# Two query tiles interleaved through attention, output projection and layer norm of an eight-core transformer layer

## The chip, the cores and the metric

The kernel runs on 8 cores of one Trainium2 chip, all with the same program and different data: core c takes batch entry c // 2 and four of its eight 512-row query tiles (the even cores tiles 0, 3, 4, 7, the odd ones 1, 2, 5, 6). The cores exchange nothing. The metric is the device time of the slowest core in microseconds (us).

## The reference

```python
# x: (4, 4096, 2048); tiers of 4, 8 and 12 heads of 64
Q_all = x @ W_Q
K_all = x @ W_K
V_all = x @ W_V
# tiers 0 and 1 add a low-rank term of rank 8 a head to K and V
scores = jnp.einsum('bhqd,bhkd->bhqk', Qh, Kh) / jnp.sqrt(jnp.float32(dk))
scores = jnp.where(causal, scores, jnp.float32(-1e+30))
attn = jax.nn.softmax(scores, axis=-1)
out = jnp.einsum('bhqk,bhkd->bhqd', attn, Vh)
a = jnp.concatenate(head_outs, axis=-1) @ W_O
x = _layernorm(x + a, axis=-1)
h = jax.nn.silu(x @ w_gate) * (x @ w_up)
x = _layernorm(x + _sparsify_2to4(h) @ w_down, axis=-1)
```

The weights are block-triangular, so that an output block of `W_O` takes only 2, 6 or 12 of the 12 head pairs. `_sparsify_2to4` keeps the two largest of each four hidden values.

## The kernel before

The program is one list of instructions for each engine, written out by Python loops. `kb.emit(engine, ..., waits, inc)` appends an instruction to its engine's list with the semaphore values that it waits for; `Buf` objects hold who wrote and who read a buffer, and give these waits. Each engine runs its list in order, so the order of the `emit` calls is the order of work. A DMA is an entry in the list of SyncE (SP) or GpSimd (POOL): it waits there, and what stands behind it in that list waits too.

Stages, with barriers between the first and second and the second and third:

1. K, V and Q for all heads by TensorE, written to HBM (`kspill`, `vspill`, `qspill`), and `wo` copied there as bf16 (`wospill`).
2. For each own tile `s` of four: attention, output projection with the residual `xTo`, layer norm (`_emit_ln`) into `x1`. Tile `s` sees `EXT[s]` = 2, 4, 6, 8 key blocks of 512. This is what the change rewrites.
3. The feed-forward part in two blocks of 1024 rows (L746 and L756 gate and up, L873 down), and the second layer norm.

Attention of a tile runs over 12 head pairs `hp` of 128 rows. A head pair is `ext` x 4 steps of 128 keys. A step is: two score matmuls (L524 and L532, one for each head, on the upper and lower 64 rows), one exp of 128x1024 on ScalarE (L547), for the last eight steps of the head pair two mask products on VectorE (L559), and two AV matmuls (L578) that add into banks 6 and 7. Their 65 rows hold 64 of the head's output and the sum of the exps.

Scores rotate through three pairs of PSUM banks (0 to 5), the exps through three buffers (`e3`). A step's AV is put in a queue, `avq`, and emitted when more than two are in it:

```python
                    avq.append(do_av)
                    if len(avq) > 2:
                        flush_av()
            while avq:
                flush_av()
```

So AV of step k - 2 stands behind the scores of step k in TensorE's list, and the scores of step k + 1 behind that. At the end of a head pair the queue is emptied, and a fixed chain follows (the hand-over): VectorE copies banks 6 and 7 (L602, L606), ScalarE takes Ln and exp(-x) of the sums (L612, L616, L622, L626), TensorE spreads the result over 128 rows (L635, L641) into the next score pair, and VectorE multiplies (L649, L656) into `ob`. The first scores of the next head pair stand behind L641 in TensorE's list.

K and V of a head pair are loaded into `kst` and `vst`, two buffers each, so that the next head pair's are on their way; Q of all heads of a tile comes in one load (`qb`), and `xTo` of the tile goes to `xos` through POOL's queue as soon as the layer norm before has been read. All loads are emitted by the helper at L230.

The output projection (L686) takes two groups of eight 128-row output blocks, one PSUM bank each. Each group runs over the head pairs `ho` with one `wospill` load of 512 KB (128x2048) into one of two slots: 6 loads for the first group, 12 for the second. VectorE then adds the eight banks to `xos` (L699). The layer norm takes sums over 16 blocks (L960, L976 on TensorE, L967 on VectorE), a short chain on one row, and 32 VectorE operations (L1072, L1080); its banks are 0 to 3.

## Time and profile before

| | |
|---|---|
| time, median of 2 runs | 6110.39 us (6107.38 to 6113.41) |
| the profiled execution's own time | 6106.46 us |
| its span, slowest core | 6104.9 us (the cores: 6046.4 to 6104.9) |
| mean granted clock of TensorE, slowest core | 0.897 |
| busy in the span: TensorE | 4793.2 us (79%) |
| VectorE | 1844.3 us (30%) |
| ScalarE | 1169.1 us (19%) |
| GpSimd | 440.7 us (7%) |

The span is what the trace covers; 1.6 us of the execution's own time lie around it. Busy time says how long an engine had an instruction running, not whether anybody waited for it. The stage that is changed runs from about 1101 to 2951 us of the span. "<-" in a row's brackets names who ended the idle time before it. A granted clock of 1.00 is 2.4 GHz, 0.50 is 1.2 GHz. In timeline rows a number after x counts merged instructions.

### The profile page before, as it was taken

How to read it: one execution, taken by the hardware profiler on the slowest of the kernel's cores; microseconds unless marked ns; L12 is line 12 of the kernel's file. 1: busy time of each engine (PE TensorE's matmuls, PEld its weight loads, DVE VectorE, ACT ScalarE, POOL GpSimd, SP SyncE). 2: the span in 40 equal slices, each digit the busy share in tenths (PEclk: the TensorE clock that was granted, in tenths of full speed). 3: DMA queues.
4: the chain of work that ended last, by engine and by line, in shares of the span. 5: the costliest groups of instructions: out<-in, count | busy, mean ns of one | idle time of the engine just before them, and what ended most of it. 6: DMA issues, size and time to landing. Idle time of an engine off the chain costs nothing.

```text
span 6104.9 us, 61933 instructions; the slowest of 8 cores (6046.4 to 6104.9 us)
## 1 busy us (share of the span) xinstructions
PE 4793.2 (79%) x20400; PEld 1825.8 (30%) x20400; DVE 1844.3 (30%) x2803; ACT 1169.1 (19%) x1301; POOL 440.7 (7%) x811
## 2 busy tenths in 40 slices
PE   0889896465766766886799999788849999978894
PEld 0333333011111111111244444333314444433331
DVE  0211212434333223222444455100045445530004
ACT  0000000434626754884000000000000000000000
POOL 0000000000000000000000000122200000012220
PEclk9999998676778887988799999899969999989996
DMA  9232335322132123112344454689824455558893
GB/s 155 48 59 49 63 60 128 85 85 58 41 107 56 42 73 97 49 49 76 62 91 96 97 97 97 138 179 186 186 69 97 90 97 97 97 110 185 180 196 95
DMA packets 363871, 598.92 MB, mean 98 GB/s; under 512 B 85872, under 2 KB 208944, under 8 KB 360496
## 3 DMA queue, kind: packets, MB, share of 16 engines
q0 software_dynamic: 157488, 260.75, 27.5%
q1 hardware_dynamic: 206080, 334.21, 17.7%
q8 instruction: 180, 2.95, 0.2%
q14 instruction: 123, 1.01, 0.1%
HBM read 767.26 MB, written 88.28 MB: 140 GB/s over the span
## 4 chain that ended last, share of the span: by engine, by line
PE 52%; DMA 17%; DVE 13%; ACT 8%; issue 6%; another core or an unknown queue 2%; DVEq 0%; ACTq 0%; SPq 0%; POOLq 0%; POOL 0%
PE ps L746 15%; PE ps L756 15%; DMA ar<-wd 8%; PE ps L873 8%; ACT ar L547 6%; DMA vspill<-ar 6%; PE ps L343 4%; DVE ar L559 4%; PE ps L578 3%; DMA ar<-wospill 2%; PE ps L436 2%; PE ps L524 2%; PE ps L976 1%; PE ps L686 1%
## 5 line engine op out<-in xcount | busy, mean ns | idle before, releaser
L746 PE MATMUL ps<-ar 128*128 128x512 bf16 x4096 | 1221.4, 380 | 60.6 <-DMA ar<-wg 31.2
L756 PE MATMUL ps<-ar 128*128 128x512 bf16 x4096 | 1221.0, 380 | 1.1 <-DMA ar<-wu 1.1
L873 PE MATMUL ps<-ar 128*128 128x512 bf16 x4096 | 938.8, 385 | 195.8 <-DMA ar<-wd 122.9
L547 ACT ACTIVATE ar<-ps 128x1024 bf16<-128x1024 f32 x960 | 911.4, 1067 | 290.7 <-PE ps L532 231.7
L578 PE MATMUL ps<-ar 128*65 128x512 bf16 x1920 | 647.3, 422 | 136.1 <-DVE ar L559 135.0
L873 PEld LDWEIGHTS ps<-ar 128*128 128x128 bf16 x4096 | 391.4, 99 | 743.1 <-issue 326.1
L524 PE MATMUL ps<-ar 64*128 64x512 bf16 x960 | 419.3, 447 | 191.8 <-DMA ar<-kspill 82.1
L746 PEld LDWEIGHTS ps<-ar 128*128 128x128 bf16 x4096 | 401.3, 98 | 547.1 <-issue 65.7
L559 DVE TENSOR_TENSOR ar<-ar 128x512 bf16<-128x512 bf16 x768 | 318.1, 425 | 811.1 <-ACT ar L547 768.8
L756 PEld LDWEIGHTS ps<-ar 128*128 128x128 bf16 x4096 | 401.3, 98 | 486.9 <-issue 5.3
L776 ACT ACTIVATE ar<-ps 128x1024 bf16<-128x1024 f32 x128 | 131.1, 1024 | 1609.0 <-PE ps L746 953.0
L532 PE MATMUL ps<-ar 64*128 64x512 bf16 x960 | 420.3, 448 | 0.0
L279 DVE CAST ar<-ps 128x512 bf16<-128x512 f32 x240 | 164.8, 692 | 673.6 <-DMA vspill<-ar 386.1
L891 DVE TENSOR_TENSOR ar<-ps,ar 128x512 bf16<-128x512 f32 x64 | 44.3, 692 | 1056.9 <-PE ps L873 1050.7
L230 POOL DMA_DIRECT2D ar<-wd x512 | 270.6, 529 | 903.3 <-PE ps L873 758.4
L781 DVE TENSOR_SCALAR ar<-ar 128x1024 bf16<-128x1024 bf16 x128 | 56.6, 442 | 847.4 <-ACT ar L776 847.4
L524 PEld LDWEIGHTS ps<-ar 64*128 64x128 bf16 x960 | 87.5, 95 | 665.0 <-issue 665.0
L373 PE MATMUL ps<-ar 128*128 128x512 bf16 x1184 | 271.2, 379 | 0.0
L578 PEld LDWEIGHTS ps<-ar 128*65 128x65 bf16 x1920 | 142.4, 115 | 427.9 <-issue 427.9
L343 PE MATMUL ps<-ar 128*128 128x512 bf16 x1056 | 237.7, 380 | 0.0
L230 POOL DMA_DIRECT2D ar<-wg x128 | 67.9, 530 | 2299.9 <-PE ps L756 1707.3
L1010 ACT ACT_TABLE_LOAD x2 | 2.6, 1283 | 1191.0 <-DVE sm L1006 1191.0
(103 smaller groups left out, 2671.6 us busy)
## 6 DMA issues: line engine op xcount, KB each, us to landing
ar<-hspill SPq DMA_DIRECT2D x512, 256.0 KB, 4.7
ar<-wg POOLq DMA_DIRECT2D x128, 512.0 KB, 6.0
ar<-wu POOLq DMA_DIRECT2D x128, 512.0 KB, 8.2
ar<-wd POOLq DMA_DIRECT2D x512, 128.0 KB, 4.9
ar<-wospill SPq DMA_DIRECT2D x72, 512.0 KB, 3.4
hspill<-ar SPq DMA_DIRECT2D x128, 256.0 KB, 7.1
ar<-xT POOLq DMA_DIRECT2D x8, 2048.0 KB, 16.9
ar<-xTo POOLq DMA_DIRECT2D x8, 2048.0 KB, 15.9
```

What stands on the lines that cost most here:

```text
L230: return kb.emit(eng, lambda e, o=out_ap, i=in_ap: e.dma_start(out=o, in_=i), waits=waits, inc=sem, incval=16)
L279: lambda e, dst=dst, src=src_bank_ap: e.tensor_copy(dst, src),
L343: lambda e, b=b, m=m, kc=kc, last=last, xch=xch: e.matmul(bank(b), wkb[:, kc * 1536 + m * 128: kc * 1536 + (m + 1) * 128], xch(kc), start= ...
L373: lambda e, b=b, ts=ts, dblk=dblk, kc=kc, xch=xch: e.matmul(bank(b), xch(kc, c0=ts * 128, w=128), wvb[:, kc * 1536 + dblk * 512: kc * 1536 ...
L524: lambda e, b0=b0, sub=sub, j=j, hp=hp, kstg=kstg: e.matmul(bank(b0), kstg[0:64, j * 512 + sub * 128: j * 512 + (sub + 1) * 128], qb[0:64, ...
L532: lambda e, b0=b0, sub=sub, j=j, hp=hp, kstg=kstg: e.matmul(bank(b0 + 1), kstg[64:128, j * 512 + sub * 128: j * 512 + (sub + 1) * 128], qb ...
L547: lambda e, b0=b0, eap=eap: e.activation(eap, ps[:, b0 * 512:(b0 + 2) * 512], AF.Exp, scale=0.125),
L559: lambda e, eap=eap, midx=midx, sub=sub, hd=hd: e.tensor_tensor(eap[:, hd * 512:(hd + 1) * 512], eap[:, hd * 512:(hd + 1) * 512], A(msk_o ...
L578: st=st, ste=ste: e.matmul(bank(6 + hd, rows=65), vstg[:, 130 * c + 65 * hd: 130 * c + 65 * hd + 65], eap[:, hd * 512:(hd + 1) * 512], sta ...
L746: lambda e, bb=bb, th=th, kc=kc, s=s, wgs=wgs: e.matmul(bank(bb + th), wgs[:, kc * 128:(kc + 1) * 128], x1[:, kc * 2048 + s * 512: kc * 20 ...
L756: lambda e, bb=bb, th=th, kc=kc, s=s, wus=wus: e.matmul(bank(bb + 2 + th), wus[:, kc * 128:(kc + 1) * 128], x1[:, kc * 2048 + s * 512: kc ...
L873: lambda e, bi=bi, ft=ft, th=th, ic=ic, wst=wst, hst=hst: e.matmul(bank(bi), wst[:, ft * 128:(ft + 1) * 128], hst[:, th * 512:(th + 1) * 512],
```

## The change

The four tiles are taken as two pairs, tiles 0 and 1, then 2 and 3; the first of a pair is chain A, the second chain B, with key extents 2 and 4, then 6 and 8.

- Attention: for each head pair, K and V are loaded once, for B's extent, and used by both. While A has key blocks left, the steps alternate A, B, A, B. B's last eight steps then run alone (solo). A owns score banks 0 and 1 and output banks 6 and 7, B owns 2 and 3, and 4 and 5; in solo steps B's scores alternate between both score pairs. `avq` is now one for each chain and is emitted when more than one is in it. At the start of the solo steps A's queue is emptied.
- The hand-over, now `_finalize_hp`, is emitted for A and then for B at the end of the head pair, with the same buffers for both (`efin`, `sm32`, `rowb`); B's last AV stands behind A's.
- Q comes for one head pair at a time, two loads of 128x512 in a ring of four. The second chain has its own masks (`msk2`).
- `xTo` of both tiles goes into the space of `kst` and `vst`, so its loads wait until the pair's attention has read these, and the next pair's K and V loads wait until both layer norms have read it.
- Output projection: both tiles together, four groups of four output blocks (eight banks: four for each tile), with 12 `wospill` loads in each group, also where `ho` is past what the group needs.
- Layer norm: A's, then B's, by the same `_emit_ln`.

```diff
+    ob2_o = xos_o
+    xosr_o = kst_o
+    B["ob2"] = Buf()
+    B["msk2"] = Buf()
+    B["qr"] = [Buf() for _ in range(4)]
+    B["xos2"] = Buf()
...
-    for s in range(4):
-        ext = EXT[s]
-        ev = dma("gpsimd", "xos",
-                 xos.rearrange("p (c t) -> p c t", c=NCK),
-                 cm(xTo)[:, :, s * 512:(s + 1) * 512],
-                 waits=B["xos"].wr_waits())
-        B["xos"].note_write(ev)
...
-                   qspill[s].rearrange("h p q -> p h q"),
-                   waits=B["qb"].wr_waits() + B["qspill"].rd_waits())
...
+    for sp_ in range(2):
+        sA, sB = 2 * sp_, 2 * sp_ + 1
+        chains = []
+        for ci, (s, pair, obank, oboff, mB, moff) in enumerate(
+                ((sA, (0, 1), (6, 7), ob_o, "msk", msk_o),
+                 (sB, (2, 3), (4, 5), ob2_o, "msk2", ring_o))):
...
+            c.avq = []
+            chains.append(c)
+        for c in chains:
+            mw = B[c.mB].wr_waits()
+            dma("sync", "mk", A(c.moff, 2048), msk[2 * c.s + 0], waits=mw)
+            dma("sync", "mk", A(c.moff + 2048, 2048), msk[2 * c.s + 1], waits=mw)
...
             kpar = hp % 2
-            kstg = A(kst_o + kpar * 4096, ext * 512)
-            vstg = A(vst_o + kpar * 4160, 130 * 4 * ext)
+            kstg = A(kst_o + kpar * 4096, 4096)
+            vstg = A(vst_o + kpar * 4160, 4160)
...
-            evk = dma("sync", "k%d" % kpar, kstg,
-                      kspill[hp, :, 0:ext * 512],
+            evk = dma("sync", "k%d" % kpar, kstg[:, 0:EXT[sB] * 512],
+                      kspill[hp, :, 0:EXT[sB] * 512],
                       waits=kB.wr_waits() + B["kspill"].rd_waits())
...
-            avq = []
-
-            def flush_av():
-                fn = avq.pop(0)
-                fn()
-
-            for j in range(ext):
...
+            dma("sync", "ql%d" % qsl, qstg[:, 0:512], qspill[sA, hp], waits=qw)
+            dma("sync", "ql%d" % qsl, qstg[:, 512:1024], qspill[sB, hp], waits=())
...
+            def chain_step(c, j, sub, pair, kstg=kstg, vstg=vstg, kB=kB, vB=vB,
+                           qstg=qstg, qrB=qrB, hp=hp):
+                b0 = pair[0]
+                qoff = 0 if c.s % 2 == 0 else 512
+                w = (kB.rd_waits() + qrB.rd_waits()
+                     + B["bank"][b0].wr_waits() + B["bank"][b0 + 1].wr_waits())
...
+                er = erot[0] % 3
...
+                if j >= c.ext - 2:
+                    midx = j - (c.ext - 2)
...
+                def do_av(c=c, j=j, sub=sub, eB=eB, eap=eap, vstg=vstg, vB=vB):
+                    cc = 4 * j + sub
...
+                c.avq.append(do_av)
+                if len(c.avq) > 1:
+                    c.avq.pop(0)()
...
+            cA, cB = chains
+            for j in range(cB.ext):
                 for sub in range(4):
-                    pr = prot[0] % 3
-                    prot[0] += 1
-                    b0 = 2 * pr
-                    w = (kB.rd_waits() + B["qb"].rd_waits()
-                         + B["bank"][b0].wr_waits() + B["bank"][b0 + 1].wr_waits())
...
-                    avq.append(do_av)
-                    if len(avq) > 2:
-                        flush_av()
-            while avq:
-                flush_av()
...
-        for grp in range(2):
-            fms = list(range(8 * grp, 8 * grp + 8))
-            nho = 6 if grp == 0 else HPN
-            for ho in range(nho):
...
+                    if j < cA.ext:
+                        chain_step(cA, j, sub, cA.pair)
+                    solo = j >= cA.ext
+                    if solo and j == cA.ext and sub == 0:
+                        while cA.avq:
+                            cA.avq.pop(0)()
+                    pair = cB.pair if (not solo or (j * 4 + sub) % 2 == 0) \
+                        else cA.pair
+                    chain_step(cB, j, sub, pair)
+            for c in chains:
+                while c.avq:
+                    c.avq.pop(0)()
+                _finalize_hp(kb, B, A, bank, kb_cnt=None, c=c, hp=hp,
+                             e_o=e_o, sm32=sm32, rowb=rowb, onesr=onesr, AFv=AF,
+                             ALUv=ALU)
+
...
+        xosbufs = (A(xosr_o, NCK * 512), A(vst_o, NCK * 512))
...
+            xB = xBs[ci]
+            kvw = (B["kst"][0].wr_waits() + B["kst"][1].wr_waits()) if ci == 0 \
+                else (B["vst"][0].wr_waits() + B["vst"][1].wr_waits())
+            evxo = dma("gpsimd", "xos" if ci == 0 else "xos2",
+                       xosbufs[ci].rearrange("p (cc t) -> p cc t", cc=NCK),
+                       cm(xTo)[:, :, c.s * 512:(c.s + 1) * 512],
+                       waits=xB.wr_waits() + kvw)
+            xB.note_write(evxo)
+        for grp4 in range(4):
+            fms = list(range(4 * grp4, 4 * grp4 + 4))
+            for ho in range(HPN):
                 rsl = ho % 2
                 rB = B["ring"][rsl]
-                wst = A(ring_o + rsl * 2048, 2048)
...
+                for ci, (obx, obxB) in enumerate(((obA, B["ob"]), (obB, B["ob2"]))):
+                    for i, fm in enumerate(fms):
+                        nho_f = 2 if fm < 2 else (6 if fm < 8 else HPN)
+                        if ho >= nho_f:
+                            continue
+                        bi = 4 * ci + i
+                        w = list(rB.rd_waits())
+                        if ho == 0:
+                            w += obxB.rd_waits() + B["bank"][bi].wr_waits()
...
+                        if ho == nho_f - 1:
+                            B["bank"][bi].note_write(evx)
+                            obxB.note_read(evx)
...
+            for ci2 in range(2):
+                for i, fm in enumerate(fms):
+                    bi = 4 * ci2 + i
+                    xB = xBs[ci2]
+                    xbuf = xosbufs[ci2]
...
+        for ci, c in enumerate(chains):
+            s = c.s
+            xB = xBs[ci]
+            xbuf = xosbufs[ci]
+            _emit_ln(kb, B, bank,
...
+        for kBx in B["kst"] + B["vst"]:
+            for sname, v in (B["xos"].wr_waits() + B["xos2"].wr_waits()):
+                kBx.note_read((sname, v))
...
+def _finalize_hp(kb, B, A, bank, kb_cnt, c, hp, e_o, sm32, rowb, onesr,
+                 AFv, ALUv):
+    fo = e_o + 3072
+    fB = B["efin"]
+    b6, b7 = c.obank
+    p0, p1 = c.pair
+    fw = B["bank"][b6].rd_waits() + B["bank"][b7].rd_waits()
+    ev5 = kb.emit("vector",
```

TensorE at the first end of a head pair, tile 0, before. L524 and L532 are a step's two score matmuls, L578 AV (x2 is one step's), L635 and L641 the broadcast.

```order
L524 MATMUL ps<-ar 128x512
L532 MATMUL ps<-ar 128x512
L578 MATMUL ps<-ar 65x512 x6
L635 MATMUL ps<-rowb,onesr 128x512
L641 MATMUL ps<-rowb,onesr 128x512
L524 MATMUL ps<-ar 128x512
L532 MATMUL ps<-ar 128x512
L524 MATMUL ps<-ar 128x512
L532 MATMUL ps<-ar 128x512
L524 MATMUL ps<-ar 128x512
L532 MATMUL ps<-ar 128x512
L578 MATMUL ps<-ar 65x512 x2
```

Three steps' scores stand ahead of the first AV, and three steps' AV are left at the end.

The same place now, end of the first head pair of tiles 0 and 1. L528 and L536 are the score matmuls, L586 AV, L977 and L984 the broadcast.

```order
L528 MATMUL ps<-ar 128x512
L536 MATMUL ps<-ar 128x512
L586 MATMUL ps<-ar 65x512 x2
L977 MATMUL ps<-rowb,onesr 128x512
L984 MATMUL ps<-rowb,onesr 128x512
L586 MATMUL ps<-ar 65x512 x2
L977 MATMUL ps<-rowb,onesr 128x512
L984 MATMUL ps<-rowb,onesr 128x512
L528 MATMUL ps<-ar 128x512
L536 MATMUL ps<-ar 128x512
L528 MATMUL ps<-ar 128x512
L536 MATMUL ps<-ar 128x512
```

B's last AV (the second x2) stands between A's broadcast and B's. The scores behind it are A's first and B's first of the next head pair.

TensorE where A ends and B goes on alone, now. Before, no such place exists: inside a head pair, score pairs and single x2 alternate, two steps apart.

```order
L528 MATMUL ps<-ar 128x512
L536 MATMUL ps<-ar 128x512
L586 MATMUL ps<-ar 65x512 x4
L528 MATMUL ps<-ar 128x512
L536 MATMUL ps<-ar 128x512
L586 MATMUL ps<-ar 65x512 x2
```

The first scores are B's last beside A. Behind them x4 is B's AV of one step before and A's last AV. The next scores are the first solo step's, and the x2 behind them is AV of the step just before; from there on AV of step k - 1 stands behind the scores of step k.

SyncE's queue from the last attention load of a tile to the first of the next, before (tile 0 to tile 1).

```order
L230 DMA ar<-wospill 128x2048 x18
L230 DMA ar<-qspill 128x12x512
L230 DMA ar<-msk 128x2048 x2
L230 DMA ar<-kspill 128x2048
L230 DMA ar<-vspill 128x2080
```

The same place now, from tiles 0 and 1 to tiles 2 and 3.

```order
L230 DMA ar<-wospill 128x2048 x48
L230 DMA ar<-msk 128x2048 x4
L230 DMA ar<-kspill 128x4096
L230 DMA ar<-vspill 128x4160
L230 DMA ar<-qspill 128x512 x2
```

48 loads for two tiles stand where 18 for one stood (36 for two), and Q stands behind K and V.

## Rows read from the trace of the kernel before

**Rows 1.** The page: chain of waits by line, and the costliest group of ScalarE.
```profile
PE ps L746 15%; PE ps L756 15%; DMA ar<-wd 8%; PE ps L873 8%; ACT ar L547 6%; DMA vspill<-ar 6%; PE ps L343 4%; DVE ar L559 4%; PE ps L578 3%; DMA ar<-wospill 2%; PE ps L436 2%; PE ps L524 2%; PE ps L976 1%; PE ps L686 1%
...
L547 ACT ACTIVATE ar<-ps 128x1024 bf16<-128x1024 f32 x960 | 911.4, 1067 | 290.7 <-PE ps L532 231.7
```

**Rows 2.** Windows, PE, PEld, DVE, ACT, POOL busy; clock, DMA: attention stages, a projection.
```profile
1101.30:1318.90 217.60, 129.51 (x408) 26.36 (x408) 111.70 (x240) 122.84 (x145) 0.00 (x0) 0.69 0.15 38
...
1431.80:1738.80 307.00, 213.94 (x790) 48.76 (x790) 111.12 (x240) 211.13 (x239) 1.15 (x1) 0.80 0.17 45
...
1852.70:2247.50 394.80, 297.15 (x1174) 71.10 (x1173) 111.01 (x240) 298.76 (x335) 1.14 (x1) 0.86 0.16 49
...
2359.50:2841.40 481.90, 385.43 (x1558) 93.95 (x1558) 111.18 (x240) 386.96 (x431) 1.14 (x1) 0.88 0.16 51
...
1318.90:1377.40 58.50, 36.13 (x136) 12.90 (x136) 11.07 (x16) 0.00 (x0) 0.00 (x0) 0.91 0.59 194
```

**Rows 3.** Timeline, fourth stage: start, length, engine, line; steps after a hand-over, then steady.
```profile
2723.18 0.60 PE L524 MATMUL ps<-ar 64*128 64x512 bf16 x1
...
2723.72 1.06 PE L578 MATMUL ps<-ar 128*65 128x512 bf16 x2
...
2724.71 0.46 PE L524 MATMUL ps<-ar 64*128 64x512 bf16 x1
...
2725.36 21.20 ACT L547 ACTIVATE ar<-ps 128x1024 bf16<-128x1024 f32 x23 [0.37 <-PE ps L532]
...
2726.53 0.39 PE L524 MATMUL ps<-ar 64*128 64x512 bf16 x1
...
2726.85 0.62 PE L578 MATMUL ps<-ar 128*65 128x512 bf16 x2
```

**Rows 4.** Timeline, fourth stage: masked steps.
```profile
2707.65 2.86 ACT L547 ACTIVATE ar<-ps 128x1024 bf16<-128x1024 f32 x3 [0.52 <-DVE ar L559]
...
2708.78 2.79 DVE L559 TENSOR_TENSOR ar<-ar 128x512 bf16<-128x512 bf16 x6 [0.59 <-ACT ar L547]
...
2709.88 0.59 PE L578 MATMUL ps<-ar 128*65 128x512 bf16 x2 [0.63 <-DVE ar L559]
...
2710.40 0.39 PE L524 MATMUL ps<-ar 64*128 64x512 bf16 x1
...
2711.03 1.94 ACT L547 ACTIVATE ar<-ps 128x1024 bf16<-128x1024 f32 x2 [0.52 <-DVE ar L559]
```

**Rows 5.** Timeline, fourth stage: hand-over to the next head pair.
```profile
2714.18 0.59 PE L578 MATMUL ps<-ar 128*65 128x512 bf16 x2 [0.33 <-DVE ar L559]
...
2714.87 0.69 DVE L602 CAST ar<-ps 65x512 bf16<-65x512 f32 x1 [0.84 <-PE ps L578]
...
2716.25 0.63 ACT L612 ACTIVATE sm<-ar 1x512 f32<-1x512 bf16 x1 [3.28 <-DVE ar L606]
...
2718.89 0.58 PE L635 MATMUL ps<-rowb,onesr 1*128 1x512 bf16 x1 [4.12 <-ACT rowb L626]
...
2719.82 0.60 PE L524 MATMUL ps<-ar 64*128 64x512 bf16 x1
...
2720.56 2.86 ACT L547 ACTIVATE ar<-ps 128x1024 bf16<-128x1024 f32 x3 [1.92 <-PE ps L532]
...
2720.71 0.68 DVE L656 TENSOR_TENSOR ar<-ar,ps 64x512 bf16<-64x512 bf16 x1
```

**Rows 6.** Windows of the first output projection, columns as in rows 2.
```profile
1323.00:1335.00 12.00, 5.53 (x24) 1.85 (x22) 1.21 (x2) 0.00 (x0) 0.00 (x0) 1.00 0.51 175
...
1335.00:1342.00 7.00, 5.77 (x15) 1.75 (x16) 4.15 (x6) 0.00 (x0) 0.00 (x0) 0.55 0.47 150
...
1346.10:1373.10 27.00, 18.86 (x80) 7.09 (x80) 1.90 (x3) 0.00 (x0) 0.00 (x0) 1.00 0.66 216
```

**Rows 7.** DMA issues by line, KB of one, microseconds from issue to landing.
```profile
ar<-xTo POOLq DMA_DIRECT2D x8, 2048.0 KB, 15.9
...
ar<-kspill SPq DMA_DIRECT2D x12, 1024.0 KB, 5.5
```

More of the change, by code:

```diff
@@ L655, in build_program @@
[L655 to L668 removed]
+            qsl = hp % 4
@@ L716, in build_program @@
+    kb.raw_wait("gpsimd", [(n, kb.cnt[n]) for n in ("xos", "xos2",
+                                                     "wr0", "wr1", "wr2", "wr3")])
     kb.barrier()
```

373 lines of the change are left out of this document (182 added, 191 removed).

## The prediction

> **What bounds the kernel now.** I read the chain of waits by line first, then the windows cut at the stage ends, then the timeline around one hand-over between head pairs. The chain [rows 1] is led by the feed-forward lines L746, L756 and L873, which the change leaves alone; L547, L559, L578, L524 and wospill are what it touches. By the windows [rows 2] the four attention stages take 217.6, 307.0, 394.8 and 481.9 us, 1401.3 in all, and one output projection 58.5 us. So some 1,640 of 6,105 us can move.
>
> An attention stage is 12 head pairs, each a run of steps (two score matmuls, one exp, two AV matmuls; a mask product too in the last eight steps of a head pair). What a step costs:
> - Unmasked, clock at 2.4 GHz: 23 exps in 21.20 us, so (21.20 - 1.02)/22 = 0.92 us [rows 3]; the mean of one is 1067 ns [rows 1], so ScalarE is the limit. TensorE needs 0.32 us from scores to AV [rows 3] and 0.52 from AV to the next scores [rows 4], 0.84 in all.
> - Masked [rows 4]: an exp starts at 2707.65 and ends 1.02 later (2708.67); its mask starts at 2708.78, AV at 2709.88 (1.21 after the exp's end), the scores queued behind it at 2710.40, their exp at 2711.03. With 1.02 for that exp the loop closes: 3.38 us. AV runs two steps late, so three steps share it: 1.13 each.
> - Clock at 1.2 GHz: scores 2723.18, AV 2723.72, scores 2724.71, so 1.53 us a step, all of it TensorE [rows 3].
>
> The hand-over [rows 4, 5]: the last exp ends at 2712.97 (2711.03 + 1.94). Last AV 2714.18, copies 2714.87, Ln 2716.25, broadcast 2718.89, first new scores 2719.82, first new exp 2720.56: 7.59 us. TensorE idles 4.12 us in it and comes back at the lower clock. Sum for the fourth stage: (481.9 - 1.6)/12 = 40.0 us per head pair (1.6: first scores to first exp, and the end of the last product against the usual next exp); 7.59 + 24 x 0.92 + 8 x 1.13 = 38.7, which leaves 1.3 for restarting at the lower clock. The others leave 1.3 to 1.5 by the same sum (the first has 1.3 us more for ScalarE's table). I take 1.4.
>
> **Part 1, interleaved unmasked steps: 0.** Before, three pairs of score banks rotate; now each chain has one. Scores of a chain wait for its previous exp: end of exp + 0.11 + 0.63 to the next exp's start = 0.74 us [rows 4], while the other chain's exp covers 0.92 - 0.10 = 0.82. It fits by 0.08 us. I cost it at nothing; what hides it is that other exp. If it failed by 0.1 us a step, 384 such steps (32 x 12) would cost 38.
>
> **Part 2, interleaved masked steps: +0.6 us per head pair.** AV again runs two steps late on TensorE, but only A is masked. Masked exp to the exp after next but one: 3.38; the fourth exp follows at once: 0.92. So 4.30 for four steps, 1.075 each, 17.2 for sixteen; before, 8 x 1.13 + 8 x 0.92 = 16.4, but those eight plain steps are counted with their own stage below.
>
> **Part 3, the eight solo steps: the largest loss.** When A has run out, B's AV is queued only one step behind its scores: scores k, AV k-1, scores k+1. Behind the mask wait of AV k-1 now stand the scores of the very next step, and ScalarE waits for them. The same 3.38 us loop is shared by two steps: 1.69 each, 13.5 for eight, against 9.0 before. TensorE then works about half of the time, and whether its clock stays is the question. The nearest rows are the output projection's: 12 us with 5.53 us busy (46%) at 1.00, followed by seven at 0.55 [rows 6], while 18.86 in 27.0 us (70%) held 1.00. At 1.2 GHz the loop is 1.21 + (1.53 - 0.54) + 0.74 + 1.02 = 3.96, so 15.8 for eight. Ends 13.5 and 15.8; half is nearest to what the rows allow: 14.6.
>
> The Trainium skill (TensorE: Matmul & The Clock Gate, "A second HAM failure mode: psum-queue depth-cycling") says that short idles between groups of matmuls, with banks cycling, make the clock swing between its two levels. By it the solo part would cost 15.8; the row at 46% agrees.
>
> **Part 4, the double hand-over: 14.2 instead of two of 7.59.** From the last exp's end: A's copies start behind the last mask (0.11 + 0.93 = 1.04), and by [rows 5] the broadcast is 4.02 later (2718.89 - 2714.87), B's last AV 0.93 after that, A's products end 6.52 after A's copies began (2721.39 - 2714.87), at 7.6. B's chain starts there: scores of the next A at 7.6 + 4.95, its exp 0.74 later, at about 13.3; the next B scores need B's products, at 14.2, and their exp slips by 0.9. So 14.2, a gain of 1.0. One restart of 1.4 in place of two.
>
> **Attention.** Per head pair of two tiles, first pair of tiles: 14.2 + 1.4 + 17.2 + 14.6 = 47.4; times 12, plus 2.9 for the ends, 571.7 against 217.6 + 307.0 = 524.6: +47. Second: 14.2 + 1.4 + 32 x 0.92 + 17.2 + 14.6 = 76.8; times 12 plus 1.6: 923.6 against 876.7: +47. Together +94. K and V are read once for both tiles, but no exp waited for K or V inside a stage of before, so this gives nothing.
>
> **Part 5, start of the second pair of tiles: +10.** Its K load overwrites xTo's buffer and stands in SP's queue until both layer norms have been read out; V, Q and the next head's loads are queued behind. 1024 KB of K take 5.5 us alone [rows 7], V (1040 KB) comes beside it, Q last: between 5.5 and twice that, nearer the upper end as all are in flight together. First scores used to start at once. The first pair's start moves 260 KB more: +1.
>
> **Part 6, output projection.** Ten loads took 27.0 us [rows 6] (80 matmuls, eight for each): 2.70 a load with both slots in use. Before: 18 loads a tile, 15 x 2.70 = 40.5 of 58.5, so 18.0 for start, boundary, evacuation. Now 48 loads for two tiles, twelve of them used by no matmul: 45 x 2.70 = 121.5, + 18.0, + 3 for two low-clock restarts behind the unused loads, - 5 for unused loads running somewhat quicker, + 8 for xTo. xTo now comes right at this stage, 2 x 15.9 us of DMA [rows 7]; the first lies beside the double hand-over (A's copy may start once the last scores have read K), half of the second beside wospill. Sum 145.5 against 117.0: +28.5 per pair, +57. Ends: unused loads free and xTo hidden, 28.5 - 27.4 - 8 = -7 per pair, -14; xTo wholly in the way, 31.8 for 8, +52 per pair, +105. The four layer norms are the same.
>
> **Sum.** 94 + 11 + 57 = +162 on the profiled execution's 6106.5: 6268; on the median of 6110.4: 6272. I say 6270. The measurement tells about 2% from no change, which here is 122 us.
>
> **Rivals.**
> - Dear: the clock stays low through the solo part (24 x 1.2 = +29), the 0.08 us of Part 1 does not hold (+38), xTo is in the way (+48): 6385. For it the 0.55 row; against it that the masked steps of before, 0.84 us of TensorE's work in 1.13, held the upper clock (their scores took 0.39 us, 0.60 after the hand-over [rows 4, 5]).
> - Cheap: wospill's unused loads cost nothing and xTo hides (-70), the solo part stays at 2.4 GHz (24 x 1.1 = -26): 6174. For it the 27.0 us window at 1.00; against it that this window's DMA share was only 0.66 and still gave 2.70 a load.
> - Not slower: interleaving covers the mask wait wherever two chains or two bank pairs alternate. Interleaved masked steps 0.92 (16 x 0.155 x 24 = -60), solo steps 1.13 ((14.6 - 9.0) x 24 = -134): 6076. It decides at the place of the scores behind the masked AV: if TensorE reached them before the mask is done, it would hold. The order of instructions speaks against it.
> - The clock never rises between hand-overs: all 768 interleaved steps cost 1.53, (0.61 + 0.455) x 384 = +409, plus 29: 6700. Against it: the same matmuls per exp ran at 0.88 mean clock in the fourth stage [rows 2]. The Trainium skill's section named above would allow this too.
>
> **How the numbers follow.** Forecast 0.52 (own range 6215 to 6330); dear 0.15; cheap 0.17; not slower 0.10; low clock 0.03; 0.03 for something else. Range 6165 to 6370: it leaves out the 0.10, the 0.03 and bits of the edges. Slower by over 2% is above 6232: 0.45 of the forecast's, the dear, the low clock: 0.66. Within 2%: the cheap, the rest of the forecast and most of "not slower": 0.28. Faster: 0.06.
>
> **What would show it.** In the new profile's windows the attention of two tiles should take about 572 and 924 us; in its timeline the solo exps should come in twos every 3.4 to 4.0 us behind a wait for the mask product; one gap of some 13 us without a big exp per head pair; the chain of waits should name wospill more, 48 loads at about 2.7 us; the first scores of the second pair should wait some 10 us for K or Q. It is wrong if solo exps come every 1.1 us, if the two projections take under 240 us, or if the granted clock in attention falls under 0.7.

## The result and the profile after

The changed kernel takes 1.0194 times as long as the one before (95% interval 1.017 to 1.0219). On the 6110.4 us of before that is 6229 us, +119 us; the interval reaches from +104 to +134, so it is slower, and whether by more than 2% is open. (In many executions the cores of one die run at a lower clock; the ratio leaves these executions out, and as cores 0 to 3 did so in the profiled one of the changed kernel, the rows below are core 5's, clock 0.896, beside core 5 of before.) The forecast was 6270, +160. Direction and range hold, the size was too large by a third (160 for 119).

Page of the changed kernel, core 5: the chain of waits by line, then AV (L586, once L578).

```profile
PE ps L733 14%; PE ps L743 14%; ACT ar L551 9%; PE ps L860 8%; DMA ar<-wd 7%; DMA vspill<-ar 6%; PE ps L343 4%; DMA ar<-wospill 3%; DVE ar L564 2%; PE ps L586 2%; PE ps L436 2%; PE ps L528 1%; PE ps L659 1%; PE ps L1037 1%
...
L586 PE MATMUL ps<-ar 128*65 128x512 bf16 x1920 | 628.2, 411 | 219.6 <-DVE ar L564 211.5
```

The same AV line of before:

```profile
L578 PE MATMUL ps<-ar 128*65 128x512 bf16 x1920 | 647.3, 422 | 136.1 <-DVE ar L559 135.0
```

Against [rows 1], wospill has gone from 2% to 3% and the exp (L551, once L547) from 6% to 9% of the chain, while the mask product went from 4% to 2%. That last share misleads: the column "idle before" says that TensorE waited 211.5 us for the mask product ahead of AV, where it had waited 135.0. The chain follows one path back and gives each wait to whoever released it last; how long an engine stood idle for a releaser is in the group's last column.

Windows of the changed kernel, columns as in [rows 2]: attention and output projection of tiles 0 and 1, then of tiles 2 and 3.

```profile
1094.00:1643.20 549.20, 316.25 (x1201) 74.89 (x1202) 223.85 (x478) 339.52 (x385) 2.30 (x2) 0.80 0.11 31
1643.20:1791.30 148.10, 78.52 (x274) 27.14 (x273) 23.08 (x35) 0.00 (x0) 0.00 (x0) 0.79 0.62 191
1907.60:2813.60 906.00, 667.88 (x2737) 175.50 (x2738) 223.86 (x478) 691.00 (x768) 2.28 (x2) 0.88 0.10 33
2813.60:2954.10 140.50, 72.28 (x274) 25.94 (x273) 23.04 (x35) 0.00 (x0) 0.00 (x0) 0.84 0.62 187
```

Attention takes 1455.2 us against 1401.3 [rows 2], +53.9. The projections take 288.6; the four of before were 58.5, 59.8, 58.0 and 55.7, 232.0 together, so +56.6. With the start of the second pair (+8.4, below) that is +118.9. The two spans of core 5 (6104.9 and 6199.3) differ by only 94, because code that the change leaves alone was quicker in this one execution: what stands ahead of attention by 7.3 us, and the feed-forward part by 15.6, as its window in the changed kernel and then the same window of before show.

```profile
3067.30:6079.90 3012.60, 2748.21 (x12355) 1197.33 (x12356) 965.12 (x1162) 137.44 (x135) 403.94 (x764) 0.96 0.63 126
```

```profile
2957.00:5985.20 3028.20, 2747.01 (x12356) 1198.00 (x12356) 964.86 (x1162) 137.49 (x135) 404.04 (x764) 0.96 0.62 125
```

TensorE is busy for the same time in both; only its waits differ. So stages are compared here, not spans.

That 118.9 meets the measured +119 so closely is luck, since core 5 is one core of eight. With the stages cut alike on all eight cores (a projection from its first matmul to its last residual add, which gives 288.8 and 230.8 on core 5), the means are: attention 1457.5 us against 1404.3 (+53), the projections 291.7 against 224.0 (+68), the second pair's start 8.3. That is +129 us, within the interval; the stretch from the first exp to the first feed-forward matmul grew by 127. Core 5's projections of before were among the slow ones, so that its +56.6 is too small for the chip.

**The solo steps.** Timeline of the changed kernel, second pair of tiles, where chain A has ended.

```profile
2561.22 1.95 ACT L551 ACTIVATE ar<-ps 128x1024 bf16<-128x1024 f32 x2 [1.11 <-PE ps L536]
...
2562.34 1.88 DVE L564 TENSOR_TENSOR ar<-ar 128x512 bf16<-128x512 bf16 x4 [2.37 <-ACT ar L551]
...
2563.45 0.59 PE L586 MATMUL ps<-ar 128*65 128x512 bf16 x2 [1.54 <-DVE ar L564]
...
2564.55 2.00 ACT L551 ACTIVATE ar<-ps 128x1024 bf16<-128x1024 f32 x2 [1.38 <-PE ps L536]
...
2566.77 0.59 PE L586 MATMUL ps<-ar 128*65 128x512 bf16 x2 [1.49 <-DVE ar L564]
...
2567.92 1.02 ACT L551 ACTIVATE ar<-ps 128x1024 bf16<-128x1024 f32 x1 [1.38 <-PE ps L536]
```

Exps come in twos at 2561.22, 2564.55 and 2567.92: 3.33 and 3.37 us apart, with TensorE idle for 1.5 us in each for the mask product. This is the forecast's 3.38 us loop shared by two steps. The windows of the same place tell what the clock did: solo steps, the last of them, the hand-over, the restart, and steady steps.

```profile
2561.20:2571.20 10.00, 5.28 (x24) 1.28 (x22) 5.02 (x12) 6.00 (x6) 0.00 (x0) 1.00 0.00 1
2571.20:2574.20 3.00, 2.17 (x6) 0.43 (x6) 0.91 (x3) 2.05 (x2) 0.00 (x0) 0.55 0.27 38
2574.20:2587.60 13.40, 3.92 (x9) 0.55 (x8) 5.20 (x9) 4.58 (x8) 0.00 (x0) 0.50 0.45 171
2587.60:2592.10 4.50, 3.36 (x10) 0.75 (x10) 0.85 (x2) 3.57 (x4) 0.00 (x0) 0.51 0.00 0
2592.10:2610.00 17.90, 17.90 (x80) 5.21 (x80) 0.00 (x0) 17.71 (x20) 0.00 (x0) 1.00 0.00 0
```

The granted clock stays at 1.00 (2.4 GHz) through 10 us in which TensorE is busy for 5.28, and falls to half only in the last two solo steps. Such windows over the solo parts of all twelve head pairs of this stage read 1.00 to the start of the last exp in eight of them and 0.92 to 0.96 in four. It can go otherwise: the kernel without the unused loads (below) has the same attention code, and one of its twelve solo parts of tiles 2 and 3 fell early:

```profile
2121.30:2135.40 14.10, 10.19 (x31) 2.03 (x30) 5.83 (x14) 7.07 (x7) 0.00 (x0) 0.64 0.00 1
```

There the scores start every 2.02 us (2128.53, 2130.54, 2132.57), and the solo part takes 15.2 us. Two of the 24 solo parts of the kernel with xTo cut short do the same (0.60 and 0.65; 15.3 and 15.0 us). The lower level is rare in this place, not excluded.

**The hand-over.** Timeline of the changed kernel from the last exp of one head pair to the first exps of the next.

```profile
2573.14 1.02 ACT L551 ACTIVATE ar<-ps 128x1024 bf16<-128x1024 f32 x1 [0.81 <-PE ps L536]
...
2575.14 0.68 DVE L944 CAST ar<-ps 65x512 bf16<-65x512 f32 x1
...
2579.14 0.58 PE L977 MATMUL ps<-rowb,onesr 1*128 1x512 bf16 x1 [4.58 <-ACT rowb L971]
...
2581.96 0.69 DVE L944 CAST ar<-ps 65x512 bf16<-65x512 f32 x1 [0.31 <-DVE ar L1000]
...
2585.98 0.58 PE L977 MATMUL ps<-rowb,onesr 1*128 1x512 bf16 x1 [4.83 <-ACT rowb L971]
...
2587.65 1.02 ACT L551 ACTIVATE ar<-ps 128x1024 bf16<-128x1024 f32 x1 [1.82 <-PE ps L536]
...
2589.45 3.07 ACT L551 ACTIVATE ar<-ps 128x1024 bf16<-128x1024 f32 x3 [0.77 <-PE ps L536]
```

The last exp ends at 2574.16 and the next starts at 2587.65, 13.49 us later. A's copies start at 2575.14 and B's at 2581.96: one chain of copy, Ln, exp, broadcast and product behind the other. The second exp starts 1.80 after the first, where steady exps start every 0.92: the forecast's slip of 0.9.

The starts of all 960 big exps, averaged over the twelve head pairs of each pair of tiles, give the parts of a head pair (each up to the end of its last exp, but the 32 unmasked steps up to the start of the exp behind them):

| us per head pair | forecast | measured, tiles 0, 1 | measured, tiles 2, 3 |
|---|---|---|---|
| hand-over, without a big exp | 13.3 | 13.54 | 13.54 |
| 32 unmasked steps with slip and restart | 31.7 | none | 31.23 |
| 16 interleaved masked steps (tiles 0, 1: with slip and restart) | 17.2 (19.5) | 18.79 | 17.45 |
| 8 solo steps | 14.6 | 13.33 | 13.28 |
| sum | 47.4 and 76.8 | 45.66 | 75.50 |

**The second pair's start.** Timeline: the last product of the layer norms, the issue of the K load, the first scores.

```profile
1898.36 0.69 DVE L1141 TENSOR_TENSOR ar<-ar,ps 128x512 bf16<-128x512 bf16 x1
...
1899.18 0.33 SPq L230 DMA_DIRECT2D ar<-kspill  x1
...
1907.62 0.58 PE L528 MATMUL ps<-ar 64*128 64x512 bf16 x1 [33.91 <-DMA ar<-qspill]
```

From the issue to the first scores 8.4 us, and Q, the last of the three, is what they wait for.

### The profile page after: what moved, and what is told of

Its sections match the earlier page's. It is cut to its first block, busy times and chain, and to the rows that moved or that the text cites. A ratio compares the mean times of both kernels' runs of the same rounds, so it can differ in the third digit from the quotient of the medians.

```text
span 6311.9 us, 62057 instructions; the slowest of 8 cores (6177.1 to 6311.9 us)
## 1 busy us (share of the span) xinstructions
PE 4924.5 (78%) x20400; PEld 1879.4 (30%) x20400; DVE 1849.5 (29%) x2803; ACT 1176.5 (19%) x1301; POOL 446.3 (7%) x811
## 3 DMA queue, kind: packets, MB, share of 16 engines
q14 instruction: 124, 1.02, 0.1%
## 4 chain that ended last, share of the span: by engine, by line
PE 54%; DMA 16%; ACT 11%; DVE 11%; issue 5%; another core or an unknown queue 2%; DVEq 0%; ACTq 0%; SPq 0%; POOLq 0%; POOL 0%
PE ps L733 15%; PE ps L743 15%; PE ps L860 9%; ACT ar L551 9%; DMA ar<-wd 6%; DMA vspill<-ar 5%; PE ps L343 4%; DMA ar<-wospill 3%; DVE ar L564 2%; PE ps L586 2%; PE ps L436 2%; PE ps L528 1%; PE ps L659 1%; PE ps L1037 1%
## 5 line engine op out<-in xcount | busy, mean ns | idle before, releaser
L733 PE MATMUL ps<-ar 128*128 128x512 bf16 x4096 | 1276.3, 395 | 58.3 <-DMA ar<-wg 31.1
L743 PE MATMUL ps<-ar 128*128 128x512 bf16 x4096 | 1276.0, 395 | 1.0 <-DMA ar<-wu 1.0
L860 PE MATMUL ps<-ar 128*128 128x512 bf16 x4096 | 1000.7, 406 | 156.2 <-DMA ar<-wd 86.4
L551 ACT ACTIVATE ar<-ps 128x1024 bf16<-128x1024 f32 x960 | 919.0, 1050 | 290.8 <-PE ps L536 245.3
L586 PE MATMUL ps<-ar 128*65 128x512 bf16 x1920 | 633.1, 413 | 215.5 <-DVE ar L564 208.5
L860 PEld LDWEIGHTS ps<-ar 128*128 128x128 bf16 x4096 | 410.3, 102 | 746.7 <-issue 499.9
L733 PEld LDWEIGHTS ps<-ar 128*128 128x128 bf16 x4096 | 412.7, 101 | 582.6 <-issue 226.5
L743 PEld LDWEIGHTS ps<-ar 128*128 128x128 bf16 x4096 | 412.8, 101 | 524.7 <-issue 168.4
L528 PE MATMUL ps<-ar 64*128 64x512 bf16 x960 | 391.0, 412 | 142.5 <-DMA ar<-qspill 110.7
L536 PE MATMUL ps<-ar 64*128 64x512 bf16 x960 | 396.4, 418 | 0.0
L586 PEld LDWEIGHTS ps<-ar 128*65 128x65 bf16 x1920 | 140.0, 113 | 488.4 <-issue 488.4
L373 PE MATMUL ps<-ar 128*128 128x512 bf16 x1184 | 271.2, 379 | 0.0
L528 PEld LDWEIGHTS ps<-ar 64*128 64x128 bf16 x960 | 89.9, 94 | 575.4 <-issue 573.2
L659 PE MATMUL ps<-ar 128*128 128x512 bf16 x544 | 153.0, 430 | 125.2 <-DMA ar<-wospill 120.5
L343 PE MATMUL ps<-ar 128*128 128x512 bf16 x1056 | 238.1, 380 | 0.0
## 6 DMA issues: line engine op xcount, KB each, us to landing
ar<-xTo POOLq DMA_DIRECT2D x8, 2048.0 KB, 15.8
```

The costliest lines, as they stand in the source:

```text
L343: lambda e, b=b, m=m, kc=kc, last=last, xch=xch: e.matmul(bank(b), wkb[:, kc * 1536 + m * 128: kc * 1536 + (m + 1) * 128], xch(kc), start= ...
L373: lambda e, b=b, ts=ts, dblk=dblk, kc=kc, xch=xch: e.matmul(bank(b), xch(kc, c0=ts * 128, w=128), wvb[:, kc * 1536 + dblk * 512: kc * 1536 ...
L528: lambda e, b0=b0, sub=sub, j=j, qoff=qoff: e.matmul(bank(b0), kstg[0:64, j * 512 + sub * 128: j * 512 + (sub + 1) * 128], qstg[0:64, qoff ...
L536: lambda e, b0=b0, sub=sub, j=j, qoff=qoff: e.matmul(bank(b0 + 1), kstg[64:128, j * 512 + sub * 128: j * 512 + (sub + 1) * 128], qstg[64:1 ...
L551: lambda e, b0=b0, eap=eap: e.activation(eap, ps[:, b0 * 512:(b0 + 2) * 512], AF.Exp, scale=0.125),
L586: st=st, ste=ste: e.matmul(bank(c.obank[hd], rows=65), vstg[:, 130 * cc + 65 * hd: 130 * cc + 65 * hd + 65], eap[:, hd * 512:(hd + 1) * 51 ...
```

## The experiments

Kernels that ran on one chip share its runs of the kernel before. Where there is no interval, one time is given.

**AV two steps late in the solo part alone.** Edit of the changed kernel:

```diff
-                if len(c.avq) > 1:
+                if len(c.avq) > (1 if j < cA_ext else 2):
```

> The changed kernel, with B's AV queued two steps late in the solo stretch (as before) and one step late elsewhere. Theory (solo steps wait for the mask product because AV of the step just before stands ahead of the next scores): the eight solo exps come in threes every 3.4 us, the solo stretch falls from about 14.2 to 9.0 us per head pair, less 0.6 us given back at the hand-over, where two AV of B now stand behind A's broadcast instead of one; 24 x 4.6 = 110 us less than the changed kernel, about 6120, ratio to the kernel before 1.00; the two attention windows 549 and 906 us become about 494 and 851. Rival (ScalarE waits in the solo stretch because two score pairs serve one chain, or because of the clock): less than 20 us gained.

The ratio to before is 1.004 (1.0012 to 1.0067), so about 94 us of the changed kernel's +119 are gone. Windows of its two attention stages:

```profile
1045.80:1557.30 511.50, 319.82 (x1201) 77.00 (x1201) 222.09 (x478) 335.49 (x385) 2.30 (x2) 0.78 0.12 34
...
1818.00:2680.60 862.60, 666.33 (x2736) 177.31 (x2736) 222.15 (x478) 687.34 (x768) 2.28 (x2) 0.88 0.11 34
```

Attention takes 1374.1, 81 less. The solo part fell from 13.3 to 9.95 and 9.67 us, which by 24 head pairs is 84, less than the 110 expected, which went from 14.2 to 9.0; so the windows of 494 and 851 were missed by 17 and 12 us. The hand-over grew by 0.13, since one more AV is left for it. So the order of AV and scores on TensorE in the solo part is worth 81 to 94 us, and with it changed attention is already 27 us below before. The clock has little share in it: the solo parts of tiles 2 and 3 read 1.00 in eleven of twelve head pairs here (0.81 in the other), and in eight of twelve in the changed kernel.

**Without the loads that no matmul uses.** Edit of the changed kernel:

```diff
-            for ho in range(HPN):
+            for ho in range(6 if grp4 < 2 else HPN):
```

> The changed kernel without the 24 wospill loads that no matmul uses (six loads in groups 1 and 2, as the blocks need). Theory (each load has its 2.7 us, used or not): the two projections (148 and 141 us) lose 12 x 2.2 to 2.7 us each, in all 53 to 65 us, about 6170, ratio 1.010. Rival (unused loads run at once beside the banks' evacuation and cost little): under 20 us, ratio 1.016 or more.

Windows of the two projections:

```profile
1609.90:1729.30 119.40, 75.59 (x274) 26.18 (x273) 23.00 (x34) 0.00 (x0) 0.00 (x0) 0.90 0.63 184
...
2753.10:2871.10 118.00, 73.26 (x274) 26.05 (x273) 23.02 (x34) 0.00 (x0) 0.00 (x0) 0.90 0.58 168
```

237.4 against 288.6: 51 us for 24 loads, 2.1 us each. Over all eight cores the means are 235.6 against 291.7 (289.9 and 291.1 in the two kernels with AV later, which kept these loads): 54 to 56 us, 2.3 each. The matmuls are the same 274 records, and the clock rises from 0.79 and 0.84 to 0.90; TensorE's busy time falls by 2.9 and rises by 1.0 us, so little of the gain is faster matmuls. Its time is 6176 us. The projections are then 5 us above before's on core 5 (232.0), and 12 above them in the mean of the cores (224.0), which is what xTo costs below.

**The kernel before, with AV one step late.** It is the reverse of the first: does the lag alone, without interleaving, cost what the change's solo steps cost?

```diff
-                    if len(avq) > 2:
+                    if len(avq) > 1:
```

> The kernel before with one edit: AV is emitted one step late instead of two. Theory: each of its 384 masked steps costs 1.69 instead of 1.13 us, unmasked steps are covered; 384 x 0.56 = 215 us, less about 0.9 us at each of 48 hand-overs, where one AV fewer is left: about +170 to +215, the first attention stage 217.6 us goes to about 265. Rival (one step late is enough, the loss comes from interleaving itself): within 20 us of the kernel before.

One time, 6407 us, beside 6094 to 6134 of before on its chip: about +290 where +170 to +215 were expected. Core 5's four attention stages take 307 us more. Windows of the first and the fourth attention stage:

```profile
1084.90:1357.00 272.10, 146.15 (x408) 28.18 (x408) 112.83 (x240) 125.73 (x145) 0.00 (x0) 0.58 0.10 29
...
2548.40:3135.20 586.80, 389.39 (x1558) 94.46 (x1558) 113.09 (x240) 408.03 (x431) 1.14 (x1) 0.88 0.13 42
```

The first, all masked, is +54.5 against 217.6. Part of that is the clock, which reads 0.58 here and 0.69 in [rows 2]; the masked steps of one head pair of the first stage and of one of the fourth:

```profile
1131.20:1146.20 15.00, 10.18 (x28) 2.01 (x26) 6.71 (x16) 8.07 (x8) 0.00 (x0) 0.50 0.01 2
...
2624.50:2636.80 12.30, 6.40 (x28) 1.65 (x28) 5.79 (x14) 8.06 (x8) 0.00 (x0) 1.00 0.03 5
```

The fourth stage is +104.9 against 481.9, and masked steps alone would make it grow no more than the first. Its timeline at unmasked steps shows the rest:

```profile
2661.42 1.94 ACT L547 ACTIVATE ar<-ps 128x1024 bf16<-128x1024 f32 x2 [0.32 <-PE ps L532]
...
2662.58 0.59 PE L578 MATMUL ps<-ar 128*65 128x512 bf16 x2 [0.43 <-ACT ar L547]
...
2663.11 0.39 PE L524 MATMUL ps<-ar 64*128 64x512 bf16 x1
...
2663.68 1.94 ACT L547 ACTIVATE ar<-ps 128x1024 bf16<-128x1024 f32 x2 [0.32 <-PE ps L532]
```

Two exps every 2.26 us, 1.13 each instead of 0.92: AV k - 1 waits for its exp, the scores k + 1 stand behind it, and the loop (the first exp ends at 2662.44; 0.14 to AV, 0.53 to the scores, 0.57 to their exp, 1.02 for it: 2.26) is shared by two steps. The expectation that unmasked steps are covered with a lag of one was wrong. In the changed kernel they are covered (0.92) although each chain's queue holds one, since between a chain's scores and its AV the other chain's step stands: on TensorE AV is two steps late again.

**The kernel before with two pairs of score banks instead of three.** It tests Part 1 alone:

```diff
-                    pr = prot[0] % 3
+                    pr = prot[0] % 2
...
-            pr = prot[0] % 3
+            pr = prot[0] % 2
```

> The kernel before with one edit: scores rotate through two pairs of banks instead of three. Theory (an exp frees its banks 0.08 us before it matters): unmasked and masked steps keep 0.92 and 1.13 us; only the start of a head pair loses its third score pair: 0 to 0.5 us x 48, so 0 to +25 us. Rival (the third pair carries the unmasked steps): 0.1 us or more on each of 576 unmasked steps, +58 us or more, seen in the fourth stage (481.9 us) as +20 us or more.

One time, 6142 us. Windows of the first and the fourth attention stage:

```profile
1074.60:1293.40 218.80, 129.01 (x408) 27.49 (x408) 112.27 (x240) 123.89 (x145) 0.00 (x0) 0.70 0.14 37
...
2325.70:2815.70 490.00, 392.60 (x1558) 102.02 (x1558) 111.28 (x240) 389.01 (x431) 1.14 (x1) 0.88 0.16 50
```

+1.2 and +8.1, about 12 over all four stages. The third pair was slack, as Part 1 has it. Of the 0.7 us that a head pair of the fourth stage loses, 0.6 lie in its first six steps, where the third score pair is missed; the later unmasked steps still start every 0.90 to 0.94 us, so the margin of 0.08 us holds.

**xTo loads cut short.** Of the changed kernel's two loads of 2048 KB only the first of 16 blocks is read; for the other 15 the projection adds no residual from `x`.

```diff
-                       xosbufs[ci].rearrange("p (cc t) -> p cc t", cc=NCK),
-                       cm(xTo)[:, :, c.s * 512:(c.s + 1) * 512],
+                       xosbufs[ci][:, 0:512],
+                       xTo[0:128, c.s * 512:(c.s + 1) * 512],
```

> The changed kernel with each xTo load of stage 2 cut to one of its 16 blocks (the residual is then not added for the others; all else is left). Theory (xTo shares the DMA engines with wospill for about half of its second load): each projection loses 5 to 12 us, 10 to 24 in all. Rival 1 (xTo lies wholly in the way): 25 us or more a projection. Rival 2 (hidden beside the double hand-over): under 3 us a projection.

Windows of the projections:

```profile
1614.70:1752.00 137.30, 72.59 (x274) 26.04 (x273) 22.98 (x34) 0.00 (x0) 0.00 (x0) 0.84 0.57 191
...
2775.90:2917.00 141.10, 72.98 (x274) 26.11 (x273) 23.05 (x35) 0.00 (x0) 0.00 (x0) 0.84 0.51 171
```

Against 148.1 and 140.5 that is -10.8 and +0.6; single projections of equal code differ by 8 us. The means of eight cores are steadier: 280.1 us for the two against 289.9 to 291.7 in the three kernels with full xTo loads. That is 10 to 12 us, 5 to 6 a pair of tiles, where Part 6 had 8, and neither nothing nor wholly in the way. One time, 6212 us.

**AV two steps late in each chain, with eight exp buffers.** Edit of the changed kernel (AV later keeps exps longer, so their ring grows from three to eight):

```diff
-                er = erot[0] % 3
+                er = erot[0] % 8
...
-                if len(c.avq) > 1:
+                if len(c.avq) > 2:
```

> The changed kernel with eight exp buffers instead of three, and AV two steps late in each chain (so four steps late overall while two chains run). Theory: interleaved masked steps fall from 1.08 to 0.92 us (16 x 0.16 = 2.5 us a head pair) and the solo stretch from 13.3 to about 9.7 as in the run with two steps in the solo stretch alone; 24 x 6.0 = 145 us less than the changed kernel, about 6085, ratio 0.996. Rival (the masked interleaved steps are held by VectorE or by the score banks, not by AV's place): no better than that other run, ratio 1.004.

The ratio is 0.998 (0.9945 to 1.0016). Windows of its attention:

```profile
1061.40:1555.00 493.60, 323.05 (x1200) 81.56 (x1200) 222.45 (x478) 332.42 (x385) 2.30 (x2) 0.76 0.12 35
...
1818.10:2666.80 848.70, 678.49 (x2737) 183.42 (x2738) 222.43 (x478) 683.85 (x768) 2.28 (x2) 0.86 0.11 35
```

Interleaved masked steps fall from 17.45 to 14.79 us for sixteen, 0.92 each: ScalarE never waits for a mask there. Tiles 0 and 1 gain less (18.79 to 17.10), since they restart inside these steps. Attention is 1342.3, 59 below before, and the projections, the unused loads above all, give it back: the ratio is 1.

**A's hand-over inside the solo steps.** On top of eight buffers and without the unused loads, A's copies follow the first solo step, its Ln and exp the second, its broadcast the fifth, which goes into A's own output banks:

```diff
+                    si = (j - cA.ext) * 4 + sub
+                    if si in (0, 1, 4):
+                        fin(cA, part={0: 0, 1: 1, 4: 2}[si])
...
-            for c in chains:
-                while c.avq:
-                    c.avq.pop(0)()
...
+            while cB.avq:
+                cB.avq.pop(0)()
+            fin(cB)
```

> As the run with eight exp buffers, without the unused wospill loads, and with A's hand-over emitted inside B's solo stretch (copies after the first solo step, Ln and exp after the second, broadcast into A's own output banks and products after the fifth). Theory: the gap without a big exp falls from 13.5 to 7.6 us, given back 2.4 us of ScalarE for the four small operations and up to 1 us of stalls: 24 x 2.7 to 3.5 = 65 to 85 us, and 57 for the loads: about 5950, ratio 0.974. Rival (the small operations delay the solo steps by as much as the gap shrinks): only the loads' 57 us, ratio 0.987.

One time, 6039 us, beside 6078 to 6120 of the version above on the same chip: the 40 to 80 us are about what the unused loads cost, and the hidden hand-over gave next to nothing. It ran again on another chip, for a trace to read:

> The version with A's hand-over inside the solo stretch again, for its profile. Its one undisturbed time was 6039 us, which is the run with eight exp buffers less the loads' 57 us and nothing more. Theory 1 (the gap did shrink, and the solo stretch grew by as much): the gap without a big exp is about 8 us instead of 13.7 and the solo stretch about 15 instead of 10.2, with one interval of 3 us or more where ScalarE does the four small operations and one where it waits for A's broadcast behind them on TensorE. Theory 2 (the gap did not shrink): still 13 us or more.

Timeline of the second run, start of a solo part:

```profile
1920.19 1.94 ACT L551 ACTIVATE ar<-ps 128x1024 bf16<-128x1024 f32 x2 [1.44 <-PE ps L536]
...
1921.31 0.96 DVE L564 TENSOR_TENSOR ar<-ar 128x512 bf16<-128x512 bf16 x2 [2.42 <-ACT ar L551]
...
1922.19 0.68 DVE L951 CAST ar<-ps 65x512 bf16<-65x512 f32 x1
...
1923.56 0.63 ACT L964 ACTIVATE sm<-ar 1x512 f32<-1x512 bf16 x1 [1.43 <-DVE ar L956]
...
1925.85 2.88 ACT L551 ACTIVATE ar<-ps 128x1024 bf16<-128x1024 f32 x3
...
1930.72 1.02 ACT L551 ACTIVATE ar<-ps 128x1024 bf16<-128x1024 f32 x1 [1.98 <-PE ps L536]
```

VectorE gets to A's copies (1922.19) only behind the first solo mask (1921.31); ScalarE, in order, stands at A's Ln until 1923.56 and runs four small operations, so that the next big exp starts at 1925.85, 4.73 us after the one before it. The hand-over fell from 13.7 to 7.76 and 7.98 us, and the solo part rose from 10.24 to 16.1. Attention takes 1346 us on core 5, against 1342.3 of the version above: the wait was moved, not hidden.

**B's hand-over moved into the next head pair.** On top of that, B's last AVs, copies, Ln and broadcast are emitted behind the first three steps of the next head pair's B:

```diff
+                    if pend and j == 0 and sub < 3:
+                        pend[0](sub)
...
+            pend.append(later)
```

> As the run before, and B's last AV and hand-over are emitted inside the next head pair (AV and copies after its first two steps, Ln and exp after the fourth, broadcast and products after the sixth). Theory: the gap of 7.6 us falls to about 1, given back 2.4 of ScalarE; the clock does not fall at a head pair's end, which saves the restart of about 1; 24 x 5 = 120 us: about 5830, ratio 0.954. Rival (the clock falls anyway and the new stalls eat the gain): ratio 0.97.

> The last version again, timed in more rounds. Its one undisturbed time was 5922 us beside 6089 to 6124 for the kernel before: ratio 0.966 to 0.972.

The first run gives one time, 5922 us, beside 6089 to 6123 of before on its chip; the second has a ratio of 0.9725 (0.9675 to 0.9774). A head pair takes 35.34 us in tiles 0 and 1 and 64.93 in 2 and 3, against 45.66 and 75.50: where a double hand-over of 13.5 us stood, ScalarE is now without a big exp for 0.7 us, with one interval of 3.14 us behind it, where the moved Ln and exp stand. Attention falls from 1346 to 1219.5 us on core 5, about the 120 us expected of this step; the time of 5830 was missed, because it was counted from a version at 0.974, and that one came to about 0.99 (6109 us beside 6143 to 6184).

**A's copies ahead of the first solo step.** The remaining 4.73 us come from VectorE's order by the reading above, so the copies go ahead of the step whose mask they waited for:

```diff
                         while cA.avq:
                             cA.avq.pop(0)()
+                        fin(cA, part=0)
...
-                    if si in (0, 1, 4):
-                        fin(cA, part={0: 0, 1: 1, 4: 2}[si])
+                    if si in (0, 4):
+                        fin(cA, part={0: 1, 4: 2}[si])
```

> As the version with both hand-overs moved, but A's copies are emitted ahead of the first solo step and Ln and exp right after it (before, the copies stood behind the first solo step's mask product on VectorE, and ScalarE's next exps stood behind Ln). Theory: the interval of 4.7 us in the solo stretch (seen in the profile with A's hand-over moved) falls to about 3.3 (0.92 + 2.4 for the four small operations), and the later one of 3.0 us, where TensorE waits for A's broadcast, to about 1.5; 24 x 2.5 to 3 = 60 to 70 us, ratio 0.962 against 0.9725. Rival (ScalarE waits there for the masked steps' AV, not for the copies): no change, 0.97.

The ratio is 0.9658 (0.9624 to 0.9693), 5901 us on 6110.4. Windows of its attention stages and projections:

```profile
1058.60:1477.10 418.50, 331.44 (x1201) 83.02 (x1202) 220.06 (x478) 333.42 (x385) 2.30 (x2) 0.79 0.13 39
1477.10:1594.90 117.80, 72.85 (x274) 25.70 (x273) 23.16 (x35) 0.00 (x0) 0.00 (x0) 0.91 0.67 197
...
1711.60:2473.40 761.80, 673.09 (x2737) 182.16 (x2738) 221.73 (x478) 683.28 (x768) 2.28 (x2) 0.91 0.11 37
2473.40:2594.20 120.80, 74.70 (x274) 26.08 (x273) 23.16 (x35) 0.00 (x0) 0.00 (x0) 0.88 0.60 172
```

The interval of 4.73 us is 3.35, and a head pair takes 34.18 and 62.94 us. That is 38 us in all, against 60 to 70 expected: a later interval, 3.0 us with A's hand-over alone moved, was to fall to about 1.5 and still reads 2.48 in tiles 0 and 1 and 1.77 in tiles 2 and 3. Attention is 1180.3 us against 1401.3 before and 1455.2 after the change, with ScalarE busy for 1016.7 of it (333.42 + 683.28). This version beats both kernels.

## Why the prediction was right or wrong

**Right: the direction, the range, and where the time goes.** Attention, the projections and, by 8 us, the second pair's start grew, and nothing else did. That the sum missed by only 41 us is in part luck: in the mean of eight cores attention was forecast 41 us too dear (94 for 53) and the projections 11 too cheap (57 for 68).

**Part 1, nothing for the interleaved unmasked steps: held.** They come 0.92 us apart once the clock is up; two bank pairs in before cost 12 us over all four stages, most of it at the start of a head pair. The margin of 0.08 us was enough.

**Part 2, 17.2 for sixteen interleaved masked steps: held, 17.45.** With AV later still the wait is gone (14.79), so it was this wait and not ScalarE.

**Part 3, 14.6 for eight solo steps: mis-sized, 13.3.** The loop of 3.38 us, shared by two, was right to 0.05 us, and the experiment that changes only the lag takes it away. What failed is the choice of the middle between 13.5 and 15.8: "half is nearest to what the rows allow" took the projection's row at 46% with 0.55 after it [rows 6] as the nearest. The solo part is busy for 5.28 of 10.00 us at 1.00, and in this trace of core 5 the clock falls, where it does, only near its end (the lowest of the 24 solo parts reads 0.86). Of the two ends the upper one was worked out rightly (2.02 us a step at 1.2 GHz for 1.98); it is the rare case, and half a weight was too much for it. That is 1.3 us in each of 24 head pairs: 31 of the 40 us by which attention was too dear on core 5. The Trainium skill (TensorE: Matmul & The Clock Gate, "A second HAM failure mode: psum-queue depth-cycling") had the clock swing in such groups with short idles. The traces agree in few solo parts: 15.0 to 15.3 us, near the 15.8 due by it, in three of 48 of the two kernels named above, while eight of twelve of tiles 2 and 3 in this one stayed at 1.00.

**Part 4, the double hand-over: held.** 13.3 and the slip of 0.9 were forecast, 13.54 measured; in the rows above, copy to copy is 6.82, where the steps gave 6.52 and left out the 0.31 that the second copy's row shows. The restart was mis-sized: slip and restart together were to cost 2.3 and cost 1.8 in tiles 2 and 3 (31.23 - 32 x 0.92) and 1.3 in tiles 0 and 1 (18.79 - 17.45). The 1.4 was a remainder of sums over before's stages, not a row; what it holds besides the clock was not tried. By the table the rows that hold the restart are 0.5 us (31.7 for 31.23) and 0.7 us (19.5 for 18.79) below the forecast, 15 of the 40 us; the stages' ends are 3 more, and hand-over (0.24 in 24) and interleaved steps (0.25 in 12) give 9 back: 31 + 15 + 3 - 9 = 40. K and V read once gave nothing that any row shows.

**Part 5, +10: 8.4.** Right, with Q last.

**Part 6, +57: +56.6 on core 5, +68 in the mean of the cores.** The level of 145.5 us a pair was right (291.7 for the two); the base was not: 58.5, the first projection of core 5, stood for all four, and over the eight cores their mean is 56.0. The unused loads are 51 to 56 us, 2.1 to 2.3 each, less than the 2.70 a load of the projection and as the forecast had them with its -5; xTo is 10 to 12, 5 to 6 a pair for the 8 forecast.

**Rivals.** "Dear" needed a low clock in the solo part, which came in few, and xTo in the way, which was 5 to 6 us a pair: fell. "Cheap" lies below the result: its solo part at 2.4 GHz was right for most, its free loads were not. "Not slower" put masked steps at 0.92 interleaved and 1.13 solo wherever two chains alternate. It fell for this kernel, and the lag experiments show its condition: with AV one step later in TensorE's order the same interleaving gives 0.92 and 1.28 (10.24/8). The low clock fell: 0.88 in the attention of tiles 2 and 3.

**Errors in the expectations.** With a lag of one in the kernel before I costed only masked steps; unmasked ones lose 0.21 each too. And moving A's hand-over to where its data is ready did not hide it, since two in-order queues, VectorE's and ScalarE's, passed the wait on.

## What to carry to other kernels

Count the lag of a pipelined product in the engine's own order of instructions, not in the length of a chain's queue: a queue of one beside a second chain is a lag of two, and becomes a lag of one when that chain ends. When a dependent sequence is moved beside other work, move each engine's part to the place where its input is there and nothing of the new neighbour's stands ahead of it; otherwise the gap comes back as a gap inside the neighbour. A load whose data nobody uses still took its slot here, 2.1 to 2.3 us each, so a loop bound shared by groups of unequal length is worth a look.
